# Attention over the last keys: the value products of two steps made together in each second step, with five buffers for probabilities

## The reference

```
x = x + gelu(LN(x) @ ctx^T) @ ctx                 # stage 1, per batch, ctx has 1601 rows
x = x + experts(LN(x))                            # stage 2, top tokens of 8 experts
q = LN(x) @ Wq.T ; k = ctx @ Wk.T ; v = ctx @ Wv.T        # stage 3: 16 heads of 16
scores = q k^T + bias[bucket(distance)] ; scores = where(mask, scores, -1e9)
x = x + (softmax(scores) @ v) @ Wo.T
x = x + 0.3 * (expert_of_batch(x) @ Wo2 + bo)             # stage 4
```

## Time and profile before

| what | us |
|---|---|
| runs (3) | 666.12, 666.88, 671.56; median 666.88 |
| the profiled execution, its own time | 669.96 |
| its span, first to last instruction | 668.1 |
| PE busy | 619.4 (93%) |
| DVE busy | 328.3 (49%) |
| ACT busy | 264.4 (40%) |
| POOL busy | 121.8 (18%) |
| granted TensorE clock, mean | 0.984 of full speed |

### The profile page before, as it was taken

One profiled execution on the slowest core, in us unless ns is written; L12 is line 12 of the kernel. 1 busy time (PEld: TensorE's weight loads), 2 busy tenths in 40 slices (PEclk: granted clock), 3 DMA queues, 4 the chain that ended last, 5 costly groups with the idle time before them and its releaser, 6 DMA issues.

```text
span 668.1 us, 9082 instructions
## 1 busy us (share of the span) xinstructions
PE 619.4 (93%) x3053; PEld 381.4 (57%) x3055; DVE 328.3 (49%) x1041; ACT 264.4 (40%) x362; POOL 121.8 (18%) x178
## 2 busy tenths in 40 slices
PE   3999999999999768799999878999999999999998
PEld 1666666666666535699998533334434433336665
DVE  4243330300301687423322967687887887834301
ACT  0211111111111334234442456767676678584321
POOL 0000000000001000254661026230041040043410
PEclk9999998999989899999999979999999999999999
DMA  9992600731400432434223894352551500041141
GB/s 313 358 366 93 206 0 1 253 95 63 130 0 1 150 114 73 131 99 134 95 72 104 237 154 64 41 80 48 104 86 40 98 1 3 2 128 47 41 134 65
DMA packets 50632, 70.53 MB, mean 106 GB/s; under 512 B 7568, under 2 KB 39226, under 8 KB 50186
## 3 DMA queue, kind: packets, MB, share of 16 engines
q1 hardware_dynamic: 48538, 64.45, 35.6%
q0 software_dynamic: 2048, 5.51, 2.8%
HBM read 48.22 MB, written 15.13 MB: 95 GB/s over the span
## 4 chain that ended last, share of the span: by engine, by line
PE 77%; DVE 12%; DMA 4%; issue 3%; ACT 2%; POOL 1%; DVEq 0%; POOLq 0%; ACTq 0%; SPq 0%
PE ps L928 14%; PE ps L939 14%; PE ps L1499 8%; PE ps L1481 6%; PE ps L1388 6%; PE ps L1106 6%; PE ps L1114 5%; PE ps L1225 4%; PE ps L1237 3%; DVE arena L2198 3%; DVE arena L1909 3%; PE ps L1150 2%; PE ps L1411 2%; PE ps L915 1%; DMA arena<-arena 1%
## 5 line engine op out<-in xcount | busy, mean ns | idle before, releaser
L1728 ACT ACTIVATE arena<-ps 100x1024 f32<-100x1024 f32 x128 | 123.9, 1021 | 54.6 <-PE ps L1481 54.4
L2198 DVE TENSOR_REDUCE arena<-ps 128x1 f32<-128x400 f32 x256 | 129.5, 564 | 27.4 <-PE ps L1388 25.6
L928 PE MATMUL ps<-xnT,arena 128*128 128x512 f32 x208 | 101.7, 614 | 0.9 <-DVE xnT L1793 0.9
L1535 ACT ACTIVATE arena<-ps 128x512 f32<-128x512 f32 x52 | 31.1, 597 | 176.0 <-PE ps L928 176.0
L939 PE MATMUL ps<-arena 128*128 128x256 f32 x416 | 100.2, 385 | 0.0
L939 PEld LDWEIGHTS ps<-arena 128*128 128x128 f32 x416 | 80.9, 194 | 33.6 <-issue 24.8
L1388 PE MATMUL ps<-arena 97*128 97x400 bf16 x256 | 75.8, 341 | 3.8 <-DMA arena<-arena 2.3
L1481 PE MATMUL ps<-arena 100*100 100x512 bf16 x256 | 76.2, 381 | 1.9 <-DMA arena<-arena 0.7
L1499 PE MATMUL ps<-arena 100*32 100x512 f32 x512 | 69.1, 604 | 0.0
L1388 PEld LDWEIGHTS ps<-arena 97*128 97x128 bf16 x256 | 20.4, 98 | 75.2 <-DVE arena L2198 47.0
L1793 DVE COPY xnT<-ps 128x512 f32<-128x512 f32 x16 | 10.4, 687 | 100.9 <-PE ps L901 100.9
(11 more groups left out here) (239 smaller groups left out, 688.6 us busy)
## 6 DMA issues: line engine op xcount, KB each, us to landing
arena<-in_W SPq DMA_DIRECT2D x16, 512.0 KB, 9.6
arena<-in_ctxT SPq DMA_DIRECT2D x4, 1664.0 KB, 8.2
arena<-in_ctxN SPq DMA_DIRECT2D x4, 1664.0 KB, 12.6
arena<-arena SPq DMA_DIRECT2D x48, 128.0 KB
last_k_parts<-arena SPq DMA_DIRECT2D x24, 100.0 KB, 1.8
arena<-last_k_parts SPq DMA_DIRECT2D x8, 300.0 KB
x_tok<-in_x SPq DMA_DIRECT2D x4, 512.0 KB, 9.4
xn_rows<-xn SPq DMA_DIRECT2D x4, 512.0 KB
```

Source lines behind the costliest of these rows:

```text
L928: ins = pe.matmul(ps[:, 4 + k % 2, :], ctxT_s[:, b % 2, c, f * P:f * P + P], xnT[:, c, S * b:S * b + S], start=(c == 0), stop=(c == KC - 1))
L1535: act.activation(hid[:, k % 4, :], ps[:, 4 + k % 2, :], ACT.Gelu_apprx_tanh).then_inc(s_a, 1)
L1728: act.activation(pexp2[0:KT, c % 4, :, :], ps[0:KT, 2 + 2 * (c % 2):4 + 2 * (c % 2), :], ACT.Exp).then_inc(f_pe, 1)
L2198: dve.tensor_reduce(nm2[:, m // MU % 2, h, j:j + 1], ps[:, FAST.bank(x), 0:KF], AX.X, ALU.max, negate=True).then_inc(s_by["dve"], 1)
```

## The change

The value products leave the odd steps. In each even step from 2 on, and after the last step, those of the two steps before are made one after the other: 16 matmuls in a row. So many exponentials are then unread at a time that a fifth buffer is needed: `qf_a`, which held the float copies of the first two later queries. These copies get other places (`query_floats`): six uses on four places as before, but the last two use the places of the third and fourth. The exponentials go round five buffers (`probs2(c % 5)`), wait on `f_pv` with 5 in place of 4, and the first to use `qf_a` waits until the first two queries are split.

```diff
+        def query_floats(use):
+
+            return qf_of[use] if use < 4 else qf_of[use - 2]
+
+        def probs2(n):
+            return pexp2[:, n, :, :] if n < 4 else qf_a
...
-                    if st >= 1:
-                        i, tv = divmod(st - 1, CT)
+                    for sv in (st - 2, st - 1) if st >= 2 and st % 2 == 0 else ():
+                        i, tv = divmod(sv, CT)
                         bv = i // NG
-                        c = 2 * (st - 1)
+                        c = 2 * sv
...
                             ins = pe.matmul(ps[VW * j:VW * j + VW, 6, :], V2[0:KT, bv % 2, tv, i % NG * HG + j, :],
-                                            pexp2[0:KT, (c + j // 2) % 4, j % 2, :],
+                                            probs2((c + j // 2) % 5)[0:KT, j % 2, :],
...
                     if use >= 4:
-                        act.wait_ge(s_qs, use - 3)
-                    act.activation(qf_of[use % 4], ps[:, 2 + 2 * (b % 2) + m, :], ACT.Copy, scale=a128[:, b:b + 1]).then_inc(s_qf, 1)
+                        act.wait_ge(s_qs, use - 1)
+                    act.activation(query_floats(use), ps[:, 2 + 2 * (b % 2) + m, :], ACT.Copy, scale=a128[:, b:b + 1]).then_inc(s_qf, 1)
...
-                        if c >= 4:
-                            act.wait_ge(f_pv, (c - 4) // 2 + 1)
-                        act.activation(pexp2[0:KT, c % 4, :, :], ps[0:KT, 2 + 2 * (c % 2):4 + 2 * (c % 2), :], ACT.Exp).then_inc(f_pe, 1)
+                        if c == 4:
+                            act.wait_ge(s_qs, KC)
+                        if c >= 5:
+                            act.wait_ge(f_pv, (c - 5) // 2 + 1)
+                        act.activation(probs2(c % 5)[0:KT, :, :], ps[0:KT, 2 + 2 * (c % 2):4 + 2 * (c % 2), :], ACT.Exp).then_inc(f_pe, 1)
...
-                f = qf_of[use % 4]
+                f = query_floats(use)
```

More of the change, by code:

```diff
@@ L1700, in take_product @@
                 act.wait_ge(s_made, FAST.made(x))
-                act.wait_ge(s_qs, use - 3)
-                act.activation(qf_of[use % 4], ps[:, FAST.bank(x), :], ACT.Copy, scale=a128[:, b:b + 1]).then_inc(s_by["act"], 1)
+                act.wait_ge(s_qs, use - 1)
+                act.activation(query_floats(use), ps[:, FAST.bank(x), :], ACT.Copy, scale=a128[:, b:b + 1]).then_inc(s_by["act"], 1)
                 act.wait_ge(s_by["act"], FAST.taken(x)[1])
```

## The result

The changed kernel took 693.50 us (median of four runs, 690.28 to 696.13) where the kernel before took 668.63 on the same chip. The prediction said 681.2, at most 689. The direction was right, the size was not: +25 us in place of +14.3.

What follows compares the result with a forecast made beforehand. It took TensorE and VectorE as both nearly full in the attention steps; losses of 6.4 (second and third batches), 4.4 (first), 1.1 (fourth) and 2.4 (tail) made +14.3 us, giving 681.2 us against the median 666.88; range 670 to 689.

Steps and rivals of the forecast that it cites:

- Sixteen matmuls in 1.85 us: Double value block on TensorE: 0.99 + 0.86 = 1.85 us, if the second group's weights load behind the first.
- The rival that weights of the second group are not hidden: Value blocks: up to eight loads of 0.11 us at each of 32 blocks; near 695 us, chance 0.08.
- The drain of 0.24: TensorE entering and leaving a value block costs some 0.24 us; every second one is removed.
- The score loop, 5.56: Plain pair of steps: second even-step score pair waits for ScalarE's exponential; 5.56 us for 5.30, 0.26 lost.
- Pairs with turns and roots: Pairs to 24, 26, 28, 34: VectorE frees banks late; 6.27, 6.90, 6.27, 6.10 us, +0.7 or +0.8 each.
- The four filled pairs, +0.3 a batch: Pairs with an output projection or turn of rows in the odd step: -0.2, +0.1, +0.1, +0.3, together +0.3 us.
- In plain pairs that costs nothing: The even step's second exponential waits for half the value block, 1.12 us after its start; no cost in plain pairs.
- but what stands behind it on ScalarE is late: ScalarE work behind the waiting exponential is delayed, such as step 8's query piece, copied 2.04 us after the block starts.
- The pair to 10, 7.81: From step 8's value block to step 10's: late query copy, then GpSimd's split; 7.81 us for 5.88, +1.9.
- After the table loads, +1.3: Step 48: ScalarE's two table loads, 1.28 us each, stand behind the late exponential; +1.3 us.
- the late query copy: Step 8's query piece, copied late on ScalarE, delays the turn in step 10: +1.9 us.
- switches worth 7.7 us: Attention steps: 32 entries and exits of value blocks removed, 0.24 us each, 7.7 us saved.

Runs made afterwards that it cites:

- e9: Changed kernel with a sixth probability buffer, exponentials of 256 of 512 queries and maxima over 200 of 400 keys: 662.70 us, ratio 0.9897.
- c9: Kernel before the change, with exponentials of 256 of 512 queries and maxima over 200 of 400 keys: 660.43 us, ratio 0.9852.
- e2: Changed kernel with a sixth probability buffer, so the even step's second exponential waits for no value product: 681.62 us, ratio 1.0191.
- e4: Changed kernel, five buffers, with ScalarE's copies of an even step ahead of that step's second exponential: 684.33 us, ratio 1.0232.
- e6: Changed kernel with a sixth probability buffer and maxima over only 200 of 400 keys: 671.62 us, ratio 1.0024.
- e8: Changed kernel with the value products of steps 0 and 1 made singly, in steps 1 and 2, later ones in pairs: 690.93 us, ratio 1.0310.
- e5: Changed kernel with a sixth probability buffer and exponentials of only 256 of 512 queries: 681.16 us, ratio 1.0153.

## Why the prediction was right in sign and wrong in size

- **Sixteen matmuls in 1.85 us**: right. V at 466.97 and the next maximum product at 468.82. The rival that weights of the second group are not hidden (near 695) gives nearly the time measured, but not by its mechanism. The right number was no evidence for it. The step it rests on is refuted by the row.
- **The drain of 0.24**: right in size, seen only where both other engines are light (e9's plain pairs 5.12, c9's 5.36). TensorEngine Tiling (Array Packing), Key Properties, of the Trainium skill says that a change of mode drains TensorE. The rows agree; c9 against e9 shows that the pairs with roots lose more than it gives.
- **The score loop, 5.56**: right (5.56 to 5.63 in e2 and e4). In the changed kernel it is seen only where no transfer waits.
- **Pairs with turns and roots**: right to 0.1 or 0.2 (6.96 for 6.90, 6.01 for 6.10, 6.39 and 6.43 for 6.27). e6 shows that it is VectorE's reductions that set them.
- **The four filled pairs, +0.3 a batch**: mis-sized, 1.1 (27.88 for 26.79 before). This is most of the 1.0 by which the second batch missed.
- **"In plain pairs that costs nothing" and "but what stands behind it on ScalarE is late"**: the step of the layout that failed. The exponential itself costs nothing (e4). The second half was applied to the query piece of step 8, to step 48 and to the last row of maxima, and not to every unit's copy of the turned maxima, which stands behind the same exponential, with a transfer of 2.2 us and the first scores of the next unit behind it. Before, 1.9 us were waited for it, after 9.3; in the pair to 16 it makes 6.38 of 5.56, and in the pairs to 12 and 16 together it costs 1.5. The even step of each unit holds both, so it should have been seen with the order of ScalarE in front of me, which shows L1703 just behind L1738.
- **The pair to 10, 7.81**: mis-sized, 8.25. The copy started 2.42 after V, not 2.04. The exponential was released 1.50 after V began, not 1.12, there (1.27 in the step above).
- **The clock**: a term that the sum left out, and the largest part of the miss. It costs 1.65 us in the pair to 4 (8.35 for 6.70 in e2) and 3.57 in the pair to 12 (9.91 for 6.34 in e8, whose wait and late transfer are the same), 5.2 together. The drop in the pair to 50 costs about 1.0, an estimate: from the first scores of step 50 to its V 2.61 us pass (580.68 to 583.29), and 1.64 in e4 at the full clock (571.05 to 572.69). The wait before the second drop was foreseen, its effect on the clock wasn't. How much of this a given execution pays is partly chance, as e8 shows.
- **After the table loads, +1.3**: measured 2.3 (8.79 for 6.47), of which about 1.0 is the clock drop. The rest agrees with the prediction, and e2, where the exponential is not late, has 6.49.

The miss: from V to V the changed kernel has 25.2 us more than the kernel before, 24.3 without the added group, where 14.3 were predicted. Of these 10.0 us the clock is 6.2, the transfer in the pairs to 12 and 16 1.5, the filled pairs of the second batch 0.8, the pair to 10 0.4; the rest, about 1, is spread.

The distance to e2: 12.4 us of span. 1.5 of them are there before the V of step 2 (413.32 and 411.77; e4, alike up to there, has 412.32), so they are no part of the cause. Of the 10.9 behind it (212.3 less 201.4) 5.2 are the first two drops, 2.1 the pair to 10, 2.3 the pair to 50 with the third drop, 2.4 the transfer in the pairs to 12, 16 and 60 (0.71, 0.82 and 0.84), and 1.7 go off for e2's own drop: 10.3, the rest is spread. That e2 took 681.6, near the 681.2 predicted for five buffers, is partly chance: e2 lacks the 1.9 that the late query copy was to cost, and has more in the filled pairs and by its drop.

## What to carry to other kernels

Making a block rarer and longer saves a switch only where its neighbours have buffers for the block's whole length; here three banks of maxima and two pairs of banks of scores did not, by the waits and by the cuts of e5, e6 and e9 (no run gave it more banks). With six buffers the stretch became 11.7 us longer, although switches worth 7.7 us by the prediction's count were gone. When an instruction becomes late, go down its engine's order and ask of everything behind it, in every period of the loop and not only where extra work stands, which transfer and which other engine hangs on it. Before a wait of some 2 us is put on TensorE, ask what comes next at a lower clock.

## What the runs showed of the hardware

- The granted clock fell to its lower level after a wait of TensorE of 1.4 us (step 2, in the changed kernel and e4) and one of 1.98 us (step 10), and did not after that of step 2 in e2, nor after that of step 10 in e8 (1.00 up to 460 there). In e2 it fell in the V of step 44 behind waits of only 0.60 and 0.68 us. The trace of one execution can't tell the cost of such a drop from the wait; another execution of a near kernel could (6.34 against 9.91 us). The Trainium skill, TensorE: Matmul & The Clock Gate, What's actually happening, says that one kernel makes a different number of matmuls at the lower clock from run to run, counted at a kernel's start. The traces here show it for near kernels and in mid-kernel: the pair to 12 ran at the lower clock in the changed kernel and at the full one in e8.
- The release of the exponential that waits for the first half of a block of sixteen came 1.19 to 1.50 us after the block began at the full clock (1.19 without a turn of maxima ahead of it, 1.27 with one, 1.50 in step 8), and not the 1.12 of the prediction.
